# Half-position state-space scans: later weighing of neighbouring states and drives made two at a time

## The reference, cut to what is computed

```
dA = jnp.exp(dtt[..., None] * A)
h = h * dA + (dtt * ut)[..., None] * bt[:, :, None, :]
y = jnp.einsum('bkdn,bkn->bkd', h, ct)
```

## Time and profile before

| | us |
|---|---|
| median of 3 runs | 5608.47 |
| runs from, to | 5602.5, 5612.73 |
| profiled execution, its time | 5607.85 |
| its span (first to last instruction) | 5606.0 |
| six stages of half-position scans, sum | 3252.3 |

### The profile page before, as it was taken

The page is one execution under the profiler, slowest core; times in us unless marked ns, Lnnn a source line. Parts: engine busy times, 40 slices in busy tenths (PEclk is TensorE's granted clock), DMA queues, the critical chain, the costliest instruction groups (busy, mean ns, idle before and its releaser), DMA issues. The chain is left out here.

```text
span 5606.0 us, 73119 instructions
## 1 busy us (share of the span) xinstructions
PE 4828.6 (86%) x23205; PEld 3411.3 (61%) x23205; DVE 4445.6 (79%) x4529; ACT 3634.0 (65%) x5725; POOL 3960.4 (71%) x3074
## 2 busy tenths in 40 slices
PE   7888797789898887888989888888998988888998
PEld 5776546656666645555666645565666654556777
DVE  6889838959999848977999957996999975896544
ACT  5666455448887757767878857775878865775222
POOL 5888619839999818857999935894999962984111
PEclk9999999989999998998999999998999999999999
DMA  5777607737877616647788724654877842562110
GB/s 206 263 252 264 211 10 258 252 132 254 287 268 268 226 34 219 224 135 250 260 280 271 269 69 171 220 183 161 281 266 276 271 166 102 201 216 93 43 43 29
DMA packets 356676, 1104.83 MB, mean 197 GB/s; under 512 B 33210, under 2 KB 121126, under 8 KB 354872
## 3 DMA queue, kind: packets, MB, share of 16 engines
q1 hardware_dynamic: 356280, 1100.06, 56.9%
HBM read 1086.24 MB, written 13.68 MB: 196 GB/s over the span
## 5 line engine op out<-in xcount | busy, mean ns | idle before, releaser
L1157 PE MATMUL banks<-ident,prod 128*128 128x128 f32 x4752 | 764.9, 287 | 392.5 <-DVE prod L1458 286.6
L1157 PEld LDWEIGHTS banks<-ident,prod 128*128 128x128 f32 x4752 | 556.8, 145 | 799.1 <-DVE prod L1458 557.8
L1449 DVE TENSOR_TENSOR_SCAN banks<-banks,h 128x512 f32<-128x512 f32 x594 | 723.3, 1218 | 85.8 <-ACT banks L1297 48.5
L1400 POOL TENSOR_TENSOR h<-lane,Bb 128x512 f32<-128x512 f32 x576 | 722.8, 1272 | 57.8 <-DMA Bb<-half_rows 33.8
L1297 ACT ACTIVATE banks<-lane,A 128x512 f32<-128x512 f32 x864 | 581.1, 686 | 251.6 <-DVE prod L1458 82.4
L1229 PE MATMUL banks<-w_a,Cb 128*128 128x384 f32 x1536 | 552.2, 488 | 0.0
L1449 DVE TENSOR_TENSOR_SCAN banks<-banks,half_carry_a,h 128x512 f32<-128x512 f32 x396 | 505.5, 1277 | 8.8 <-ACT banks L1297 4.9
L1400 POOL TENSOR_TENSOR h<-half_du_a,Bb 128x512 f32<-128x512 f32 x384 | 482.7, 1275 | 14.8 <-DMA Bb<-half_rows 10.1
L1297 ACT ACTIVATE banks<-half_delta_a,A 128x512 f32<-128x512 f32 x576 | 385.3, 685 | 151.5 <-DVE lane L1430 73.7
L1217 PE MATMUL banks<-big,w_a 128*128 128x256 f32 x1728 | 435.0, 394 | 1.0 <-DMA w_a<-w_in 0.8
L1458 DVE TENSOR_TENSOR prod<-banks,half_C_a 128x512 f32<-128x512 f32 x528 | 365.3, 692 | 73.4 <-DMA half_C_a<-half_rows 2.4
(11 more groups left out here) (471 smaller groups left out, 12291.6 us busy)
## 6 DMA issues: line engine op xcount, KB each, us to landing
Bb<-half_rows SPq DMA_DIRECT2D x576, 512.0 KB, 4.3
C_first<-rows SPq DMA_DIRECT2D x288, 512.0 KB, 5.4
Cb<-half_rows SPq DMA_DIRECT2D x288, 512.0 KB, 4.4
w_a<-w_in SPq DMA_DIRECT2D x256, 576.0 KB, 6.1
w_b<-w_in SPq DMA_DIRECT2D x128, 576.0 KB, 6.2
half_C_a<-half_rows SPq DMA_DIRECT2D x128, 512.0 KB, 6.7
Bb<-rows SPq DMA_DIRECT2D x96, 512.0 KB, 5.5
half_C_b<-half_rows SPq DMA_DIRECT2D x64, 512.0 KB, 6.6
```

What stands on the lines that cost most here:

```text
L1157: mm = eng.matmul(ps[:, 0, at], src[:, at], m.ident[:, :], start=n == 0 and k == 0, stop=added(s) == (i + 1) * N, is_transpose=True, skip_ ...
L1400: eng.tensor_tensor(m.dBu[:, s % DRIVES, :], m.du[i % 2], m.B[b % BRING][:, cols(s % 2)], ALU.mult).then_inc(st.dbu, 1)
L1449: eng.tensor_tensor_scan(flip(to), flip(slot(s)), flip(m.dBu[:, s % DRIVES, :]), initial, ALU.mult, ALU.add).then_inc(st.scanned, 1)
```

## The change

For the six half-position stages:
- **VectorE.** The weighings of n = 0, 2, 8, 11, 14 (`FIRST_OF_TWO`, `weighed_late`) are placed behind the scan of n + 1. `delta` of the next lane stands between scan 5 and weighing 5.
- **TensorE** adds the late states one step later, and makes the delta product at n = 1.
- **GpSimd** makes the drives of two states in one 128x1024 instruction (du is read twice, the B pair as it lies). `m.dBu` becomes two buffers of a pair. The first pair is made ahead of the loop; pair b + 1 is made at the first step of pair b, and waits until the scans of pair b - 1 are done. `du` moves to n = 12, ahead of that step's drive.
- The waits on the drives' count (`st.dbu`) count pairs, in the loads of B, `magnitude` and `scan`.
- The third `held` tile gets room of its own (`half_more`). The set of states that GpSimd weighs is the same, written as a list (`POOLED`).

```diff
-    SLOTS, DRIVES, PRODS, HELD, BRING = 4, 3, 3, 3, 3
+    SLOTS, DRIVES, PRODS, HELD, BRING = 4, 2, 3, 3, 3
+    POOLED = (1, 4, 7, 10, 13)
...
-    BEHIND = 2
+    BEHIND, DU_AT = 2, 12
...
+    FIRST_OF_TWO = (0, 2, 8, 11, 14)
+
+    def weighed_late(s):
+        return s % N in FIRST_OF_TWO
...
                 if b >= BRING:
-                    eng.wait_ge(st.dbu, s - 2 * BRING + 2)
+                    eng.wait_ge(st.dbu, b - BRING + 1)
...
                 if s < STEPS:
-                    if not by_pool(s):
+                    if n and weighed_late(s - 1):
+                        add(s - 1)
+                    if not by_pool(s) and not weighed_late(s):
                         add(s)
...
-                    if i + 1 < LANES and n == DELTA_AT - 4:
+                    if i + 1 < LANES and n == DELTA_AT - 3:
                         dt_product(i + 1)
...
                 if i >= 2:
-                    eng.wait_ge(st.dbu, (i - 1) * N)
+                    eng.wait_ge(st.dbu, (i - 1) * PAIRS)
...
-                if s >= DRIVES:
-                    eng.wait_ge(st.scanned, s - DRIVES + 1)
-                eng.tensor_tensor(m.dBu[:, s % DRIVES, :], m.du[i % 2], m.B[b % BRING][:, cols(s % 2)],
-                                  ALU.mult).then_inc(st.dbu, 1)
+                if b >= DRIVES:
+                    eng.wait_ge(st.scanned, 2 * (b - DRIVES + 1))
+                eng.tensor_tensor(m.dBu[b % DRIVES], over_tiles(m.du[i % 2], 2),
+                                  m.B[b % BRING].rearrange("p (r l) -> p r l", r=2), ALU.mult).then_inc(st.dbu, 1)
...
+            drive(0)
             for s in range(STEPS):
                 i, n = s // N, s % N
-                drive(s)
+                if n == DU_AT and i + 1 < LANES:
+                    du(i + 1)
+                if n % 2 == 0 and s + 2 < STEPS:
+                    drive(s // 2 + 1)
                 if n >= BEHIND and by_pool(s - BEHIND):
                     weigh(s - BEHIND)
-                if n == 14 and i + 1 < LANES:
-                    du(i + 1)
...
                 if s < STEPS:
                     scan(s)
-                    if not by_pool(s):
+                    if i + 1 < LANES and n == DELTA_AT + 1:
+                        delta(i + 1)
+                    if n and weighed_late(s - 1):
+                        weigh(s - 1)
+                    if not by_pool(s) and not weighed_late(s):
                         weigh(s)
...
-                    if i + 1 < LANES and n == DELTA_AT + 1:
-                        delta(i + 1)
```

More of the change, by code:

```diff
@@ L884, in own @@
         return s - pooled(s)
-    lane_order = [a for b in range(N) for a in ([] if by_pool(b) else [b]) +
+    lane_order = [a for b in range(N) for a in ([b - 1] if b and weighed_late(b - 1) else []) +
+                  ([] if by_pool(b) or weighed_late(b) else [b]) +
                   ([b - BEHIND] if b >= BEHIND and by_pool(b - BEHIND) else [])]
@@ L922, in lane @@
         return directions[d], i % TILES, c
-    held = [m.held[:, b, :] for b in range(HELD)]
+    held = m.held
     prods = [m.prods[:, b, :] for b in range(PRODS)]
@@ L2821, in half_scan_tensors @@
                 return Named(m, B=[m.Bb[:, 0, :], m.Bb[:, 1, :], m.Cb[:, 0, :]],
[L2822 to L2823 removed]
+                             dBu=[m.h[:, k, :].rearrange("p (r l) -> p r l", r=2) for k in range(2)],
+                             held=[m.h[:, 2, cols(0)], m.h[:, 2, cols(1)], named_more],
                              prods=m.prod[:, 0:2, :].rearrange("p a (b n) -> p (a b) n", n=HALF)[:, 0:3, :],
```

19 lines of the change are left out of this document (9 added, 10 removed).

## The result

| | us |
|---|---|
| before, median (4 runs) | 5609.94 |
| after, median of 4 runs (from, to) | 5521.93 (5511.73, 5534.05) |
| ratio, with its 95% interval | 0.9846 (0.9824 to 0.9868) |
| profiled execution of after | 5521.24 |
| its six half-position stages, sum | 3164.5, before 3252.3 |

What follows compares the result with a forecast made beforehand. VectorE was taken to bound the kernel; after the change GpSimd in first-half lanes, VectorE in second: mean 28.0 plus 0.5 us for decays, 108 x 28.5 = 3078 against 3252, -174, so 5432 us, range 5365 to 5550.

Steps and rivals of the forecast that it cites:

- The limit: Six half-position stages: VectorE sets the pace, 28.9 us a first-half and 30.0 a second-half lane of the 30.1 measured.
- part 1: VectorE's weighings behind the next scan: ten a lane save 0.22 us each, 2.2 us a lane, 240 us in all.
- The open end of the bounds (0 saved): VectorE's late weighings: they save nothing if the 0.22 us belongs to writing a bank.
- rival 3: VectorE's scans: the 0.22 us belongs to every scan into a bank, so no change, 5608 us; chance 0.07.
- Part 2: GpSimd's drive of two states: 2.33 us against 2.46 for two narrow ones, saving 1.0 us a lane of GpSimd's time.
- Rival 4: GpSimd's wide drive is dearer than two narrow ones; at 2.8 us a pair the kernel slows to 5733; chance 0.06.
- Part 3: GpSimd's two pair buffers: one 0.8 us wait makes GpSimd bound the 54 first-half lanes at 28.2 us; mean lane 28.0.
- the edits with one answer: Remaining edits, not walked further; for the B loads, GpSimd's 51 us of waits stay or grow a little.
- TensorE does not yet bind: TensorE: its busy time of 27.1 us per image lane lies under the forecast lane of 28.5 us.
- Part 4: ScalarE's decays, banks freed late: about 0.5 us lost behind decay 2 in first-half lanes, taken as hidden, nothing added.
- The expected bound of 100 us: VectorE's wait for ScalarE's decays in the profile after: to stay under 100 us.
- Rival 2: ScalarE's bursts or B loads take the lead: about 0.6 us lost per burst, 29.2 us a lane, 5510 us; chance 0.17.

Runs made afterwards that it cites:

- wide_only: after with all weighings directly behind their scans again and only the drives of two states kept: 5622.56 us, ratio 1.0022 to before.
- the two kernels without GELU tables: before and after with Abs in place of GELU and no exp table reload in the half-position stages: 5554.0 and 5458.89 us.
- the fourth buffer: after with a fourth buffer for pairs of B rows in the layer-0 stages: 5474.57 us, ratio 0.9765 to before.
- late_only: before with only the late weighings and the moved delta and delta product, drives left narrow: 5567.91 us, ratio 0.9926 to before.
- weigh_first: after with GpSimd's weighing ahead of du and of the wide drive: 5569.29 us, ratio 0.9932 to before.
- late_four_B: late_only with a fourth buffer of B rows in the layer-0 stages: 5556.35 us, ratio 0.9913 to before.
- n14_direct: after with state 14 weighed directly behind its scan again, four late states left: 5519.86 us, ratio 0.9845 to before.
- after_light: after with most expert products on TensorE left out in the half-position stages: 5531.25 us, ratio 0.9864 to before.
- before_light: before with most expert products on TensorE left out in the half-position stages: 5609.24 us, ratio 1.0003 to before.

## Why the prediction was half right

**The limit, and part 1: right.** VectorE set the pace. The 0.22 us belongs to reading a scan's result at once and not to writing a bank: 1.13 us between a bank scan and the next, own-result gaps from 163 to 16 us. The open end of the bounds (0 saved) is ruled out, and rival 3 with it. The sentence of the Trainium skill in "VectorE: DVE Perf Modes", section "The DRAIN you can't avoid", that rival 3 rests on does not hold for these instructions: only their order was changed, and 0.22 us went for each pair put apart. The section behind it, "Two Vector instructions with no wait between them", says that "A held instruction starts only when every earlier Vector instruction has finished"; that one which isn't held may start earlier agrees with the trace, now for bank scans too (1.13 us to the next start, behind a scan listed with 1.22).

**Part 2: right in the length, and it missed what the length does.** The wide drive takes what was taken for it (GpSimd, after, two drives):

```profile
1881.64 4.67 POOL L1408 TENSOR_TENSOR h<-lane,Bb 128x1024 f32<-128x1024 f32 x2
```

The next instruction starts at 1886.28, so a drive has 2.32 us; the median over the stages is 2.31, where 2.33 were taken. Rival 4 is out. Its sign was there all the same: wide_only is 14 us slower than before, and the trace puts this on the gate products of the Mamba stages, which end only behind the running GpSimd instruction. The prediction had no term for them.

**Part 3 failed as a step.** It said that GpSimd bounds the first-half lanes, 28.2 us against VectorE's 26.7, or 1.5 x 54 = 81 us given up to waits for drives. Inside the stages these waits grew by 21 (by 31, from 36 to 67, between the two kernels without GELU tables). It was right that the first halves would be the bad ones: they take 30.4 us, the second halves 28.2, where with the 0.5 for decays 28.7 and 28.3 were forecast, so the whole miss stands in the first halves. But what the coupling cost there lay on the way out of GpSimd: the weighing behind a wide drive that waits for B. The prediction listed the B loads among the edits with one answer ("stay or grow a little", which was 58 to 100 us) and asked only who waits for the drive, and not who waits for the weighing queued behind it. The evictions at the end of that chain (B rows, drive, weighing, add, down product, eviction) wait 44 us more, and the fourth buffer took back 47, from evictions and drives. "TensorE does not yet bind" was true of its busy time (641 / 24 = 26.7 us a lane, under 29.3) and the wrong question: TensorE takes its work in order, and what it waits for passes on to VectorE.

**Part 4 saw the kind of loss, and put its term at nothing.** It worked out a lost race of 0.5 us behind decay 2 and then added nothing, since GpSimd's lateness was to hide it. That race is lost by 0.88 us in the lane above and in 36 of the 72 layer-0 lanes, 18 us in all, and GpSimd is not late there. But this is the smaller part. The decays' waits rise by 80 us inside the stages, 0.74 a lane: 48 in the layer-0 stages, more than half of it at scans 9, 10, 14 and 15, where about 0.2 and 0 were worked out, and 32 in the Mamba stages, which part 4 did not walk and which have table loads for a SiLU besides. The expected bound of 100 us for these waits was passed.

**The sum.** Forecast were - 174 us, measured - 88. VectorE's own saving was about 247 us (146 of self-inflicted idle time and 101 of overlap), 7 more than forecast, and the drives took 60 less than the 81. Against that stand 80 us of decays, 44 of evictions, 6 of other waits and 8 of gate products, all at nothing in the forecast. The last 15 us or so come from the reckoning: by the prediction's own spacings and its 0.5 for decays a lane before takes 29.95 us, but the 28.5 after it were set against the measured 30.1. The time still fell into the range of 5365 to 5550, and there part 3's 81 us helped by luck: they stood for losses that came elsewhere.

**Rival 2** named 5510 us and came nearer to the time, by bursts and B loads together. Its own sign, 200 us of waits for decays, did not come (148), and it knew no eviction.

**The parts do not add.** - 41 and + 14 make - 27, and together they brought - 88. What goes with the missing 61 in the rows of late_only is TensorE's longer wait for the copied sum (98 to 165 us) and its lower clock behind it; weigh_first and late_four_B, with 153 and 160 us of it, lose likewise (5569, 5556). Of the kernels with late weighings and all of the work, it is 153 to 165 us in the three in which TensorE hardly waits for GpSimd's weighing (0 to 7), and 57 to 93 in the four in which it does (64 to 134). Whether TensorE, not held up there, only comes to the sum the earlier is not shown; why narrow drives lengthen the wait stays open. So does how the decays' waits divide between table loads and banks that come free late: n14_direct shows that late bank release is part of it (148 to 125), and that giving it up costs as much.

## What to carry to other kernels

Apart from its own length an instruction can have a price for waiting for and reading the result just made (here 0.22 us), and it can be bought back by order alone; look for it as idle time before an instruction that no other engine ends. When two such instructions are merged or moved on an engine that runs in order, follow also what is queued behind the one that now waits, through each engine down to the one that sets the pace: here a late load reached VectorE's eviction through a drive, a weighing, an add and a down product, and one more buffer was worth half as much again as the whole change. What a faster engine gains is to be set against the next chain's slack, stretch by stretch; a race that comes out lost belongs into the sum, and every kind of stage has to be walked, not only the largest. An instruction made longer on GpSimd is to be checked against those of VectorE whose inputs both lie in SBUF. And a saving is the difference of two sums made the same way, not of a sum and a measurement.

## What was not expected of the hardware

- A scan that writes a PSUM bank overlaps the next scan as one into SBUF does: 1.13 us between starts (1.19 with a carried start).
- A 128x1024 multiplication on GpSimd whose one operand is read twice costs no more than one with two full operands: 2.31 us between starts (median in after), against 2.33.
- A 128x512 product on VectorE with both inputs in SBUF ended 0.54 to 0.60 us behind the end of the GpSimd instruction that was running when it began, in all 18 cases of before, wide_only, after and late_only each. With the longer drive it took 2.09 us on average where it had taken 1.23.
- TensorE, stopped for 3.0 us in a stage in which it is busy for 92% of the time, was granted 0.57 of its clock over the following 4.8 us; and with less work of its own (after_light, 521 us in 690) it had 0.81. Less work for TensorE did not make the kernel faster: before_light 1.0003 (0.999 to 1.0016) of before, after_light 5531 us against 5522.
